# Causal attention with two groups of heads in one projection, and its key-side mask applied by GpSimd after the exponential

## What is computed

```python
q_lat = (x @ Wq_down).reshape(b, t, H, L)
...
v = jnp.einsum('bthl,ld->bhtd', v_lat, Wv_up)
...
q = jnp.concatenate([q_c, _apply_rope(q_e, cos, sin)], axis=-1)
k = jnp.concatenate([k_c, _apply_rope(k_e, cos, sin)], axis=-1)
scores = jnp.einsum('bhqd,bhkd->bhqk', q, k) * scale
causal = jnp.tril(jnp.ones((t, t), dtype=bool))
scores = jnp.where(causal[None, None], scores, -jnp.inf)
att = jax.nn.softmax(scores, axis=-1)
y = jnp.einsum('bhqk,bhkd->bhqd', att, v)
...
return y @ Wc
```

## Time and profile before

| | us |
|---|---|
| median of 3 runs | 3831.38 |
| lowest and highest | 3824.28, 3849.65 |
| profiled execution, its own time | 3819.7 |
| its span, first to last instruction | 3817.6 |
| TensorE, VectorE, ScalarE, GpSimd busy | 3260.0, 2545.8, 2040.0, 1891.2 |

### The profile page before, as it was taken

How to read it: one execution, slowest core, us unless ns; L and a number is a source line. 1 busy time by engine, 2 the same in 40 slices (tenths; PEclk the granted TensorE clock), 3 DMA queues, 4 the chain that set the end, 5 groups by cost and what they waited for, 6 DMA issues and landing times. The chain is left out here.

```text
span 3817.6 us, 61247 instructions
## 1 busy us (share of the span) xinstructions
PE 3260.0 (85%) x20068; PEld 2440.9 (64%) x20068; DVE 2545.8 (67%) x3859; ACT 2040.0 (53%) x4424; POOL 1891.2 (50%) x1639
## 2 busy tenths in 40 slices
PE   1959989989996888888888888898888888999868
PEld 0649965657994666666666666666666665666544
DVE  6341146554113999999999999999999834666541
ACT  0332223233224877777777777787777423666522
POOL 0023300000232888989888988888988600000045
PEclk9879999999997999999999999999999998999965
DMA  3049820002682111111111111111111000000045
GB/s 101 2 155 335 301 93 1 1 1 96 232 307 78 34 34 43 37 34 46 34 42 51 34 48 34 35 45 34 35 45 34 23 12 15 2 2 2 3 124 170
DMA packets 133783, 263.17 MB, mean 69 GB/s; under 512 B 13872, under 2 KB 104360, under 8 KB 122952
## 3 DMA queue, kind: packets, MB, share of 16 engines
q1 hardware_dynamic: 122120, 228.06, 18.0%
q0 software_dynamic: 11328, 30.95, 2.5%
HBM read 232.46 MB, written 26.51 MB: 68 GB/s over the span
## 5 line engine op out<-in xcount | busy, mean ns | idle before, releaser
L2109 POOL TENSOR_TENSOR ssm_hc<-ssm_hs,ssm_cb 128x1024 f32<-128x1024 f32 x512 | 1205.2, 2358 | 180.5 <-PE ssm_py L2223 160.1
L2609 DVE TENSOR_TENSOR_SCAN ssm_hs<-ssm_da,ssm_pb 128x512 f32<-128x512 f32 x1024 | 1220.8, 1206 | 97.0 <-POOL ssm_hc L2109 92.0
L2223 PE MATMUL ssm_py<-ssm_hc,ident 128*128 128x256 f32 x4096 | 1071.9, 385 | 38.7 <-POOL ssm_hc L2109 38.7
L2422 ACT ACTIVATE ssm_da<-ssm_dt,ssm_an 128x255 f32<-128x255 f32 x2048 | 863.2, 498 | 190.1 <-DVE ssm_hs L2609 155.5
L2223 PEld LDWEIGHTS ssm_py<-ssm_hc,ident 128*128 128x128 f32 x4096 | 711.6, 192 | 119.7 <-POOL ssm_hc L2109 46.9
L2590 DVE TENSOR_TENSOR ssm_pb<-ssm_pb,ssm_dtu 128x512 f32<-128x512 f32 x832 | 563.6, 678 | 48.0 <-PE ssm_pb L2210 25.4
L2210 PE MATMUL ssm_pb<-ssm_bst,ssm_eyeb 96*128 96x256 bf16 x1664 | 329.0, 280 | 139.6 <-DVE ssm_hs L2609 120.5
L2210 PEld LDWEIGHTS ssm_pb<-ssm_bst,ssm_eyeb 96*128 96x128 bf16 x1664 | 134.1, 99 | 344.8 <-DVE ssm_hs L2609 242.7
L3435 DVE TENSOR_TENSOR moe_hid<-moe_pu,moe_actg 128x512 f32<-128x512 f32 x71 | 49.1, 691 | 349.1 <-PE moe_pu L3078 349.1
L3078 PEld LDWEIGHTS moe_pu<-moe_xt,moe_up 128*128 128x128 f32 x2272 | 267.0, 193 | 6.4 <-ACT moe_xt L3198 3.0
L3078 PE MATMUL moe_pu<-moe_xt,moe_up 128*128 128x128 f32 x2272 | 268.0, 277 | 1.8 <-ACT moe_xt L3198 1.8
(11 more groups left out here) (587 smaller groups left out, 5442.9 us busy)
## 6 DMA issues: line engine op xcount, KB each, us to landing
moe_up<-in_moe_up SPq DMA_DIRECT2D x72, 1024.0 KB, 7.3
ssm_cb<-ssm_c_dram SPq DMA_DIRECT2D x64, 1024.0 KB, 5.6
moe_down<-in_moe_down SPq DMA_DIRECT2D x72, 512.0 KB, 5.2
sw_wt<-in_sw_w SPq DMA_DIRECT2D x47, 192.5 KB, 2.9
moe_x_dram<-moe_tok SPq DMA_DIRECT2D x32, 128.0 KB
moe_yg<-moe_y_dram SPq DMA_DIRECT2D x16, 256.0 KB, 3.1
tok_w<-in_wd SPq DMA_DIRECT2D x4, 576.0 KB
out<-h SPq DMA_DIRECT2D x1, 2056.0 KB, 7.1
```

The source lines that it names most:

```text
L2109: nc.gpsimd.tensor_tensor(hc[:, n % 2, part_], hs[:, n % 2, part_], cb[:, q % 2, part_, :], ALU.mult).then_inc(s["hc_done"], 1)
L2223: ins = nc.tensor.matmul(sums(j), k.ident[:], hc[:, n % 2, st, :], start=False, stop=(q == QN - 1 and st == NQ_ - 1 and j % 2 == 1))
L2422: ins = nc.scalar.activation(da[:, n % 2, 2 * m + o, 1:L], dt2[:, v, j, 1:L], ACT.Exp, scale=a_n[:, d, j, st:st + 1])
L2609: nc.vector.tensor_tensor_scan(two(hs[:, n % 2, 2 * m:2 * m + 2, :]), two(da[:, n % 2, 2 * m:2 * m + 2, :]), two(pb[:, p % 4]), 0.0, ALU.m ...
```

## The change

`section_attention` becomes `section_lat`, for this one section:

- Heads are packed in pairs of groups. One projection of 128 rows makes two groups, 16 rows of each in every strip; ScalarE copies the result twice with a column of ones and zeros as scale (`take_query`, `take_key`), so that each unit's tile holds one group and zeros for the other. The bias of the key's copy puts in the row of ones that takes the maxima. The values are laid out so that each unit's result has its 16 rows where the other unit of the pair has none; `scale_values` adds two units into one tile, and the output projection and the spread run over two tiles instead of four.
- The rotation is split: VectorE multiplies by the cosine and shuffles the partners (`split`), GpSimd multiplies by the sine and adds (`turn`), for q and for k, once a pair.
- The mask L867 goes. After ScalarE's exponential GpSimd puts zeros above the diagonal by position, with one affine_select over 4 x 128 elements of each partition for every call (`cut`), and the values wait for it.
- The row mask stays, and stands before the last column scores of its call.
- Row scores run two units ahead instead of one, projections four. The values of unit u come in unit u + 1. The ring is replaced by one pair of banks for row scores, one for column scores and two single banks in turn for all else. The output projection is two pieces, c = 0 and c = 1, in different units.

The core of the diff:

```diff
-RING, NB, NE = 3, 6, 4
+NB, NE = 6, 4
...
+        if key[0] in ("s1", "s2"):
+            slot = int(key[0] == "s2")
+        else:
+            slot = 2 + small[0] % 2
+            small[0] += 1
+        n[key] = (len(n), slot, used[slot])
+        used[slot] += 1
...
+        pairs, small = ps("pairs", [P, 2, 2, BANK]), ps("small", [P, 2, BANK])
...
+        partner = [n ^ 1 if n % DH >= 8 else n for n in range(32)]
+
+        def group(u):
+            return 2 * (u % 2) + u % G // 2
...
+                def turn(pair, tile, name):
+
+                    read_out(pool, name, pair)
+                    link(nc.gpsimd.tensor_tensor(tile[:, 1, :], tile[:, 1, :], rp[:, 1, :], ALU.mult))
+                    nc.gpsimd.tensor_tensor(tile[:, 0, :], tile[:, 0, :], tile[:, 1, :], ALU.add).then_inc(s[name + "_sum"], 1)
...
+                def cut(u, jp):
+
+                    read_out(pool, "s2", u, jp)
+                    upper = ex[:, (2 * u + 1 - jp) % NE].rearrange("p o (t k) -> p (o t) k", k=2 * P)[:, :, 0:P]
+                    nc.gpsimd.affine_select(out=upper, in_=upper, compare_op=ALU.is_ge, fill=0.0, base=0, pattern=[[0, 4], [1, P]], channel_multiplier=-1).then_inc(s["cut_in"], 1)
+
                 last_token(0)
-                for u in range(U):
-                    i, g = u // G, u % G
-                    if g == 0:
-                        if i + 1 < B:
-                            last_token(i + 1)
-                        if A == 2:
-                            last_value(i)
-                    last_columns(u)
+                for u in range(-4, U):
+                    if u >= 0:
+                        cut(u, 1)
+                    if u % 2 == 1 and u + 3 < U:
+                        for x in (u + 3, u + 4):
+                            last_columns(x)
+                    if u >= 0:
+                        cut(u, 0)
+                    if u % 2 == 0 and u + 4 < U:
+                        pair = (u + 4) // 2
+                        if pair % 2 == 0 and pair // 2 + 1 < B:
+                            last_token(pair // 2 + 1)
+                        turn(pair, qt, "q")
+                        turn(pair, kt, "k")
...
+                def project(pair, name, weights):
+                    i, w = pair // 2, pair % 2
+                    dst = take(name, pair)
...
+                    row, col = 0 <= u + 2 < U, 0 <= u < U
...
+                        for o in range(2):
+                            if row and t:
+                                ins1 = nc.tensor.matmul(on_diagonal(dst1[:, o, :]), eyeb[:], maskb[:], start=False, stop=True)
...
-                    if causal:
-                        for o in range(2):
-                            if row:
-                                ins1 = nc.tensor.matmul(on_diagonal(dst1[:, o, :]), eyeb[:], maskb[:, 0, :], start=False, stop=True)
-                            if col:
-                                ins2 = nc.tensor.matmul(on_diagonal(dst2[:, o, :]), eyeb[:], maskb[:, 1, :], start=False, stop=True)
...
+                    pe.wait_ge(s["cut_in"], 2 * u + 2)
...
-                    for g in range(G):
-                        ins = nc.tensor.matmul(dst[:, 0, g:g + 1], lm[:, g].rearrange("p j w -> p (j w)"), k.ones[0:HEADS, 0:1], start=True, stop=True)
+                    for w in range(2):
+                        ins = nc.tensor.matmul(dst[:, w:w + 1], lm[:, w].rearrange("p j r d -> p (j r d)"), k.ones[0:HEADS, 0:1], start=True, stop=True)
...
-                        for g in range(G):
-                            ins = nc.tensor.matmul(dst[:, c, 0:T], wo[:, g, c * P:c * P + P], og[:, i % 2, g, :], start=(g == 0), stop=(g == G - 1))
+                    for w in range(2):
+                        ins = nc.tensor.matmul(dst[:, 0:T], wo[:, w, c * P:c * P + P], og[:, i % 2, w, :], start=(w == 0), stop=(w == 1))
...
+                    scores(u, 0)
+                    if 1 <= u <= U:
+                        values(u - 1)
                     if 0 <= u + 1 < U:
                         maxima(u + 1)
-                    if 0 <= u < U:
-                        values(u, A - 1)
-                    if A == 2 and 0 <= u + 1 < U:
-                        last_key_rows(u + 1)
-                    if 0 <= u < U and g == 3:
+                    if g == 1 and 1 <= i <= B:
+                        last_out(i - 1)
+                    if g == 2 and 1 <= i <= B:
+                        last_spread(i - 1)
+                    if g == 2 and 0 <= i + 1 < B:
+                        project_last_value(i + 1)
+                    if g == 3 and 1 <= i <= B:
+                        outward(i - 1, 0)
+                    if g == 0 and 2 <= i <= B + 1:
+                        outward(i - 2, 1)
+                    scores(u, 1)
+                    if u % 2 == 0 and 0 <= u + 4 < U:
+                        project((u + 4) // 2, "q", wq)
+                        project((u + 4) // 2, "k", wk)
+                    if g == 1 and 0 <= i < B:
+                        last_query(i)
+                    if g == 3 and 0 <= i + 1 < B:
+                        project_value(i + 1)
+                    if g == 3 and 0 <= i < B:
...
+                def take_query(pair):
+
+                    act.wait_ge(s["q_sum"], pair + 1)
+                    for r in range(2):
+                        ins = nc.scalar.activation(q[:, (2 * pair + r) % NB, :], qt[:, 0, :], ACT.Copy, scale=ind[:, r, 0:1])
+                    ins.then_inc(s["q_in"], 1)
+
+                def take_key(pair):
+
+                    act.wait_ge(s["k_sum"], pair + 1)
+                    for r in range(2):
+                        ins = nc.scalar.activation(kk[:, (2 * pair + r) % NB, :], kt[:, 0, :], ACT.Identity, bias=ind[:, r, 1:2], scale=ind[:, r, 0:1])
+                    ins.then_inc(s["k_in"], 1)
...
+                    if 0 <= u < U:
+                        weigh(u, 1)
+                    if u % 2 == 1 and 0 <= u + 3 < U:
+                        take_query((u + 3) // 2)
+                        take_key((u + 3) // 2)
+                    if g == 2 and 0 <= i < B:
+                        weigh_last_query(i)
                     if 1 <= u <= U:
-                        invert(u - 1)
-                    if 0 <= u < U and g == 2:
-                        weigh_last_query(i)
+                        take_values(u - 1)
+                    if 2 <= u <= U + 1:
+                        invert(u - 2)
+                    if g == 2 and 0 <= i + 1 < B:
+                        take_last_value(i + 1)
                     if 0 <= u < U:
-                        take_values(u, A - 1)
-                    if A == 2 and 0 <= u + 1 < U:
-                        weigh_last_key(u + 1)
+                        weigh(u, 0)
...
-                def take_projections(u):
-
-                    b = u % NB
-                    done(dve, "q", u)
-                    src = bank("q", u)
-                    nc.vector.tensor_tensor(q[:, b, :], src[:, 0, 0:T], rp[:, 0, :], ALU.mult)
-                    released(nc.vector.stream_shuffle(t1[:], src[:, 0, 0:T], partner), "q", u)
-                    read_out(dve, "q", u)
-                    link(nc.vector.tensor_tensor(t1[:], t1[:], rp[:, 1, :], ALU.mult))
-                    nc.vector.tensor_tensor(q[:, b, :], q[:, b, :], t1[:], ALU.add).then_inc(s["turned_in"], 1)
-                    done(dve, "k", u)
-                    released(nc.vector.scalar_tensor_tensor(out=kk[:, b, 0, :], in0=bank("k", u)[:, 0, 0:T], scalar=ind[:, 2:3], in1=rp[:, 2, :], op0=ALU.add, op1=ALU.mult), "k", u)
...
+                def split(pair, tile, name):
+
+                    done(dve, name, pair)
+                    if pair:
+                        dve.wait_ge(s[name + "_in"], pair)
+                    src = bank(name, pair)[:, 0:T]
+                    nc.vector.tensor_tensor(tile[:, 0, :], src, rp[:, 0, :], ALU.mult)
+                    released(nc.vector.stream_shuffle(tile[:, 1, :], src, partner), name, pair)
...
+                    dst = og[:, i % 2, w, 0:256]
+                    ins = nc.vector.scalar_tensor_tensor(out=t1[:] if r else dst, in0=os_[:, u % 3, :], scalar=ind[:, r, 0:1], in1=rc[:, u % 2, :], op0=ALU.mult, op1=ALU.mult)
+                    if r:
+                        link(ins)
+                        ins = nc.vector.tensor_tensor(dst, dst, t1[:], ALU.add)
+                    ins.then_inc(s["og_in"], 1)
...
+                    row = 0 <= u + 2 < U
+                    if row:
+                        row_maxima(u + 2, 0)
                     if 0 <= u + 1 < U:
                         lower_query(u + 1)
-                    if 0 <= u < U and g == 3:
+                    if g == 0 and 1 <= i <= B:
+                        take_turned(i - 1)
+                    if g == 1 and 1 <= i <= B:
+                        take_last_out(i - 1)
+                    if g == 2 and 1 <= i <= B:
+                        take_last_spread(i - 1)
+                    if g == 3 and 0 <= i < B:
```

(16 more changed lines are left out.)

623 lines of the change are left out of this document (214 added, 409 removed).

## The result

| | kernel before | changed kernel |
|---|---|---|
| median of 4 runs | 3837.08 us | 3780.67 us |
| lowest and highest | 3824.28, 3849.65 | 3774.80, 3794.97 |
| ratio, with its 95% interval | | 0.9859 (0.9813 to 0.9904) |
| profiled execution's own time | 3819.7 us | 3782.1 us |

The change gains 56 us between the medians; the interval allows 37 to 72. The forecast was 3776 us in a range of 3748 to 3808, so time and sign were right. What follows is mostly about why: two terms of the sum were wrong by some 20 and 12 us, and others made up for most of it.

The account below looks back on a forecast made before the run. TensorE was taken to bound the loop. Instructions removed -59.2, waits -14.6, row mask +6, lateness and lock +8, start +5 summed to -55 us: 3776 us, range 3748 to 3808.

Parts of the forecast that it names:

- the tail's part: Behind the loop: 8 matmuls of the output projection go from the tail, 2.6 us less.
- Projections, output projection, spread: TensorE's loop: half of each goes, saving 26.9 us for q and k, 11.8 for output, 3.8 for the last query.
- the ring's 14.6: TensorE's wait in the loop for a bank that row maxima still read: taken as gone, 14.6 us (0 to 22).
- Key-side mask: Score calls on TensorE: two bf16 mask instructions fewer in each of 64 calls, 14.1 us less.
- Row mask inside the call: Score calls: row masks ahead of the last four column instructions cost 0.1 us a call, +6 us (0 to 13).
- Lateness and lock: Odd units of the loop: late turns and GpSimd blocking VectorE cost 0.5 us on each of 16, +8 us (0 to 27).
- TensorE's idle time: TensorE's waits in the loop: the 14.6 us wait for a bank of the ring goes, bounds 0 and 22.
- The first rival: Loop: TensorE's idle time falls as far as in section duo_, by 22 us, giving -76 us, 3755; chance 0.12.
- Start of the section: Before the loop: the longer chain from projection to first scores costs about +5 us (2 to 9).
- Single banks costing 38 us: Score calls: single banks and the longer chain lose 0.6 us in each of 64, total -17 us, 3814; chance 0.11.
- The lock turning the sum around: Cuts, turns and scalings: all 176 held 0.92 us by GpSimd and VectorE contention, change +107 us, 3938; chance 0.04.
- Code changes on GpSimd: GpSimd switching between affine_select and tensor_tensor: 64 changes of at most 6.5 us, +416 us; chance 0.01.

Follow-up runs that it names:

- e1: The changed kernel timed and profiled once more, unaltered: ratio 0.9871 against the kernel before, median 3770.96 us.
- e7: Kernel before with affine_select on the exponentials replacing the key-side mask, values in the same unit, row masks behind the columns: ratio 0.9958, loop 280.9 us.
- e3: Changed kernel with the key-side mask back on TensorE and no cut: ratio 0.9893 against the kernel before, loop 248.4 us.
- e2: Changed kernel with the row masks behind the last column scores, done signals and bank order swapped accordingly: ratio 0.9806 against the kernel before, 3743.61 us.
- e8: Changed kernel with every affine_select done twice: ratio 0.9859 against the kernel before, loop 235.3 us.
- e4: Changed kernel with the rotation's product and sum on VectorE instead of GpSimd: ratio 0.9891 against the kernel before, loop 236.9 us.
- e5: Changed kernel with folding matmuls for q and k 64 columns wide again instead of 32: ratio 0.9848 against the kernel before, section 282.1 us.
- e6: Changed kernel with row masks behind the columns and the 64-column fold: ratio 0.9805 against the kernel before, section 255.6 us.
- e10: e6 plus image 0's values projected early and turned probabilities taken ahead of row maxima: ratio 0.9776 against the kernel before, 3742.50 us.
- e9: Kernel before with the cut replacing the key-side mask and row masks ahead of the last column scores: ratio 1.0063, loop 316.1 us.

## Why the prediction was right, and where it was not

- **The sum.** Forecast -55 us; measured -56 between the medians of the first runs, -52 in e1, and -46 in the section of both profiles, which is the better measure. For the loop the steps give -59.2 + 2.6 (the tail's part) - 14.6 + 6 + 8 = -57; measured -60.2 and, in e1, -58.7. The tail gave 2.3 where 2.6 was forecast. The start took 16.5 where 5 was forecast, the loop gave 3 more than its terms, and that is the 9 us between -55 and -46. The loop is right as a total because wrong terms in it nearly cancel.
- **Projections, output projection, spread.** 26.9 and the ring's 14.6 together 41.5: measured 39.1, in one row because the wait stands behind the projection. (Counted with the piece at the loop's start it is 40.5.) Output projection 11.8: measured 10.7. Spread 3.8: measured 6.5. Right within 3 us each.
- **Key-side mask, 14.1 us.** Right: 13.1 in e7, 13.1 to 14.6 in e3.
- **Row mask inside the call, +6 us (0 to 13).** Here the step failed. It was right that the place costs something, and wrong about what and how much. The prediction saw that 128-row instructions now stand ahead of four 32-row ones, and priced it at one mask instruction. What is lost is the company of the four: they ran beside the last row scores for nothing, and alone they take 0.42 us a call. The Trainium skill describes this company (TensorE: Matmul & The Clock Gate, "Part 3: Packing small matmuls — row/col tiling": small matmuls on different 32-row strips of the array start together), and the trace agrees, with starts 0.01 us apart; what breaks it the runs show. e2 shows 26.8 us of busy time, 23 to 25 net, twice the upper bound. A better bound was in the trace: four weight loads of 0.12 us last 0.48, and as an estimate the four alone cost about that.
- **Lateness and lock, +8 us (0 to 27).** Also wrong, the other way. TensorE waited 2.6 us for exponentials in the whole loop; doubling the cut (e8) and taking the rotation off GpSimd (e4) gained or cost nearly nothing. The lock exists, as the earlier trace rows had it: the sum of two tiles takes 677 ns beside the cuts and 425 without. By the rule of the Trainium skill that the prediction weighed (SBUF — State Buffer, "Who interferes with whom") it was to be expected, and the trace agrees; but VectorE was not on the path. It also fell on another instruction than the prediction had said. Scalings of up to 1.4 us were forecast; 31 of 32 took 0.46 to 0.49. In 27 of these the scaling was under way when the cut began:

```profile
626.26 0.48 DVE L1085 SCALAR_TENSOR_TENSOR lat_t<-lat_os,lat_ind,lat_rc 128x256 f32<-128x256 f32 x1
626.41 0.83 POOL L751 TENSOR_SCALAR_AFFINE_SELECT lat_ex<-lat_ex 128x512 f32<-128x512 f32 x1 [2.89 <-ACT lat_ex L980]
626.78 0.73 DVE L1088 TENSOR_TENSOR lat_og<-lat_og,lat_t 128x256 f32<-128x256 f32 x1
```

These 27 cuts, 0.14 us behind the start of a scaling, took 0.83 to 0.85 us, the 37 others 0.63 to 0.65; the sum that began while such a cut ran took 0.73 instead of 0.43; and the one scaling that began 0.01 us behind a cut took 0.90. Whoever came second paid.
- **TensorE's idle time.** Forecast -14.6, the ring's wait. It fell from 26.6 to 7.6 us, by 19.0. The kernel before also had these waits of TensorE in its loop, which the prediction left standing:

```profile
PE lat_ring L886 <- DVEq L1138: 10.4, 9, 1.2
PE lat_ring L931 <- DVE lat_pn L1187: 4.9, 7, 0.7
```

The first stands behind the second score call, so it counts in the row "score calls"; there the masks' 14 us and these 10.4 make up for the place's 26.8 all but 2.3, and the row shows +1.1. The second stands behind the values and is half of that row's 9.8; the other half stands in the same place: in 14 more units the row scores L855 behind the values wait 3.4 us in all, for L1154's lowered query or for L1040, and where nothing waits the values take 0.79 us in both kernels. The first rival was right in direction: idle fell by 19 of the 22 us it took. (Its own rows give 25: 26.9 us idle in 292, and 0.8% of the new loop.)
- **Start of the section, +5 us (2 to 9).** Measured +16.5. Some 6 us are the fold, which I had not counted as changed at all; e5 takes them back. The other 10 are the stretch up to the first exponential: four row-score calls and two projections at a mean granted clock of 0.67 instead of 0.85, and a first chain of 7 us instead of 6. Between e6 and e10, which differ in order alone, the stretch falls from 22.6 to 18.8 us and its granted clock rises from 0.66 to 0.85, the value of the kernel before; at that clock it is 4.0 us longer than there, near the forecast 5. So a good part seems to be the clock, which the prediction left out at the start; how the 10 split between clock and work no run separates.
- **The rivals.** Single banks costing 38 us: refuted, 2.6 us of waits. The lock turning the sum around: refuted by e8. Code changes on GpSimd: where a product of a turn follows a cut it begins 0.3 us behind its end, and a cut behind a turn begins with no gap at all, so there is no change of 6.5 us.

## What to carry to other kernels

When a scheduled piece of TensorE's work is moved, ask what ran beside it: instructions on different row strips are free only while they stand next to each other, and two full-height instructions between them cost the others their cover, here 0.42 us a call and more than the edit gained in e9. Whether a term is hidden is cheaply tested by doubling it, as e8 did with the cut. And read a change of 1% from the stretch that it touches: the section repeated to 0.5 us where single profiles scattered by 18 elsewhere.

## What the runs showed of the hardware

- Two bf16 masks of 128 rows between row and column scores: the four 32x128 f32 instructions behind them take 0.42 us; next to the row scores, nothing measurable (call 1.60 against 1.19 us, e2). The two masks themselves take 0.33 us ahead of 32-row instructions (e9, 701.53 to 701.86) and 0.23 ahead of a full-size projection (e7, 693.83 to 694.06).
- affine_select over 4 x 128 of f32 in SBUF takes 0.63 to 0.65 us, and 0.83 to 0.85 where it began 0.14 us into a VectorE instruction with two SBUF inputs; 0.72 on average. A VectorE sum of two SBUF tiles that began while it ran took 0.73 instead of 0.43.
- The stretch of the 96 folding matmuls took 17.2 to 20.1 us at a granted clock of 0.54 to 0.64 with 32 columns each, and 11.9 to 12.1 us at 0.93 to 0.98 where q and k had 64 columns each. I had not expected the start of the section to have a price at all that depends on this; the runs do not tell why it does.
